# The later router joined into round 2, and the MLP's sums taken out of PSUM ahead of two convolution tiles

## The reference

```python
x = _layernorm(x + _L0_attn_ref(x, ...))   # Mamba-2 mixer, then a gated MLP
x = _layernorm(x + _L0_ffn_ref(x, ...))    # top-2 of 8 experts: softmax router, one matrix and bias each
x = _layernorm(x + _L1_attn_ref(x, ...))   # attention, 16 heads, relative positions
x = _layernorm(x + _L1_ffn_ref(x, ...))    # top-2 of 8 gated experts with a capacity of 512
```

```python
mlp = jax.nn.silu(h @ gate_w.T) * (h @ up_w.T) @ down_w.T
x = x + mlp_scale[None, None, :] * mlp
gate_scores = jax.nn.softmax(jnp.einsum('bsd,ed->bse', x, Wg) + bg, axis=-1)
topk_scores, topk_idx = jax.lax.top_k(gate_scores, 2)
```

## Time and profile before

| | us |
|---|---|
| median of 3 runs | 1363.02 |
| lowest, highest | 1362.93, 1367.55 |
| the profiled execution | 1364.65 |
| its span, first to last instruction | 1362.9 |
| the four slots that the diff touches | about 80 to 500 of the span |
| attention, then second experts | about 500 to 1363 |

### The profile page before, as it was taken

One profiled execution on the slowest core, in us unless ns is written; L12 is line 12 of the kernel. 1 busy time (PEld: TensorE's weight loads), 2 busy tenths in 40 slices (PEclk: granted clock), 3 DMA queues, 4 the chain that ended last, 5 costly groups with the idle time before them and its releaser, 6 DMA issues. The chain is left out here.

```text
span 1362.9 us, 39431 instructions
## 1 busy us (share of the span) xinstructions
PE 1224.1 (90%) x16528; PEld 648.2 (48%) x16528; DVE 1091.9 (80%) x2184; ACT 902.2 (66%) x1739; POOL 295.2 (22%) x417
## 2 busy tenths in 40 slices
PE   4988888889888778999999999999999999994995
PEld 2555445545554423555555444454445544432552
DVE  6777888989785888999999989989899998934123
ACT  5665345537513305999998888888889888891242
POOL 2222131330312015000000200601106011054471
PEclk9999989999898988999999999999999999996998
DMA  5080000200208503102122011302111200011235
GB/s 144 1 234 16 1 2 17 111 2 1 112 1 154 144 1 146 38 21 45 36 56 64 21 37 45 83 27 61 38 44 40 63 13 22 13 43 39 58 101 187
DMA packets 59703, 77.72 MB, mean 57 GB/s; under 512 B 15010, under 2 KB 41189, under 8 KB 57686
## 3 DMA queue, kind: packets, MB, share of 16 engines
q1 hardware_dynamic: 56454, 70.95, 19.4%
q0 software_dynamic: 3072, 4.25, 1.0%
HBM read 37.18 MB, written 40.03 MB: 57 GB/s over the span
## 5 line engine op out<-in xcount | busy, mean ns | idle before, releaser
L1491 ACT ACTIVATE space<-ps 128x512 f32<-128x512 f32 x1024 | 605.4, 598 | 85.9 <-PE ps L671 37.3
L2151 DVE TENSOR_REDUCE smax<-ps 128x1 f32<-128x1024 f32 x512 | 613.6, 1220 | 50.6 <-PE ps L671 26.0
L671 PE MATMUL ps<-space 96*32 96x512 bf16 (+2 forms) x8432 | 614.9, 381 | 23.3 <-DVE smax L2151 12.8
L671 PEld LDWEIGHTS ps<-space 96*32 96x32 bf16 (+2 forms) x8432 | 255.0, 98 | 286.6 <-DVE smax L2151 42.6
L1052 PE MATMUL ps<-space 128*9 128x256 f32 x4096 | 319.6, 379 | 0.0
L1052 PEld LDWEIGHTS ps<-space 128*9 128x9 f32 x4096 | 119.8, 92 | 98.1 <-ACT space L1491 1.0
L1355 ACT ACTIVATE btok<-ps 128x128 f32<-128x128 f32 x32 | 8.9, 278 | 106.1 <-issue 89.6
L2096 DVE SCALAR_TENSOR_TENSOR x<-ps,gsel,x 128x128 f32<-128x128 f32 x256 | 69.0, 342 | 8.0 <-PE ps L671 7.6
L671 PE MATMUL ps<-w_exp,xnT 128*128 128x512 f32 x128 | 63.5, 620 | 13.3 <-DVE x L2096 13.3
L1596 POOL TENSOR_SCALAR eps_sum<-mv 128x4 f32<-128x4 f32 x32 | 7.4, 233 | 314.0 <-DVEq L1867 313.3
L671 PE MATMUL ps<-ones,ident 128*128 128x512 bf16 x228 | 59.0, 419 | 17.4 <-POOLq L1707 12.3
(11 more groups left out here) (250 smaller groups left out, 1416.5 us busy)
## 6 DMA issues: line engine op xcount, KB each, us to landing
head_sums<-space SPq DMA_DIRECT2D x31, 256.0 KB
q_rows<-space SPq DMA_DIRECT2D x24, 256.0 KB, 2.5
k_rows<-space SPq DMA_DIRECT2D x24, 256.0 KB, 2.8
space<-k_rows SPq DMA_DIRECT2D x16, 384.0 KB, 5.4
space<-q_rows SPq DMA_DIRECT2D x16, 384.0 KB, 7.1
expert_out<-x_all SPq DMA_DIRECT2D x2, 2048.0 KB, 18.3
space<-expert_out SPq DMA_DIRECT2D x4, 1024.0 KB, 9.5
v_rows<-space SPq DMA_DIRECT2D x4, 576.0 KB, 3.4
```

Source lines behind the costliest of these rows:

```text
L671: return nc.tensor.matmul(out, lhsT, rhs, start=first, stop=last)
L1491: nc.scalar.activation(prob[:, QUAD * (step % PROB_SETS) + unit % QUAD, :], bank(STB + unit % 2), ACT.Exp)\
L2151: v.tensor_reduce(smax[:, N % 2, i:i + 1], ps[:, b0:b0 + 2, :].rearrange("p k n -> p (k n)"), AX.X, ALU.max).then_inc(S.s_max, 1)
```

## The change

TensorE's `route0` goes from the end of round 1 into round 2, between `chunk_state` and the next chunk's front. ScalarE's `evac_T` for the router goes ahead of `decays_so_far` in round 1. VectorE's `route_logits` and `route_shift` go from round 1 into round 2, ahead of `chunk_weights`; `route_which`, `route_picks` and `gate_parts` go ahead of `chunk_weights` in round 3, and in round 5 (`BIAS_AT`) the first `experts_scaled` does. At the MLP's end VectorE's `skip_rows` goes into the loop at n = 6, both `skip_sum` go ahead of the last two of the left convolution tiles, and the statistics go behind `chunk_inputs` of chunk 0. ScalarE's list behind the loop stays as it was.

```diff
--- before.py
+++ after.py
@@ -963,6 +963,10 @@
                         chunk_carried(m, c)
                         if c < NT - 1:
                             chunk_state(m, c)
+                    if p is not None and c == 2:
+                        route0(p)
+                    if m is not None:
+                        if c < NT - 1:
                             chunk_front(m, c + 1)
                             chunk_after(m, c + 1)
                     if p is not None and c == 1:
@@ -980,8 +984,6 @@
                         if c == NT - 1:
                             mix_out(m, 0)
                     if p is not None:
-                        if c == 1:
-                            route0(p)
                         if c == 2 and m is None:
                             keep_clock(YB, 10)
                             score_pair(0)
@@ -1432,14 +1434,14 @@
                     if m is not None and c < NT - 1:
                         chunk_copy(m, c + 1)
                         chunk_exp(m, c + 1)
+                    if p is not None and c == 1:
+                        evac_T("moe", p, (7, 5))
                     if m is not None and c + 2 < NT:
                         decays_so_far(m, c + 2)
                     if p is not None and c == BIAS_AT:
                         evac_gates(p)
                     if m is not None and c in (2, 4, 6):
                         gated_squares(m, c // 2 - 1)
-                    if p is not None and c == 1:
-                        evac_T("moe", p, (7, 5))
                     if p is not None and c == 2:
                         route_exp(p)
                     if q is not None and c < 3:
@@ -2061,7 +2063,6 @@
                 dve.wait_ge(S.down_psum, 2 * b + H + 1)
                 v.tensor_tensor(xa[:, own(H), :], xa[:, own(H), :], tiles4(5 + H), ALU.add).then_inc(S.skip_sum, 1)
                 dve.wait_ge(S.skip_sum, 2 * b + H + 1)
-                statistics(xa, H, 0)
 
             def gate_parts(b):
                 for k in range(TOPK):
@@ -2169,6 +2170,8 @@
                 for n in range(2 * HID_TILES):
                     if p is not None:
                         hidden(p, n)
+                    if p is not None and n == 2 * HID_TILES - 2:
+                        skip_rows(p)
                     if q is not None and p is not None and n == 0:
                         expert_norm(q, 1)
                     if m is not None and 2 <= n + 1 < conv_in_mlp(q):
@@ -2178,18 +2181,21 @@
                         if p is None and n == 5:
                             for pair in range(EARLY_PAIRS - 3, EARLY_PAIRS):
                                 pair_max(pair)
-                if m is not None:
-                    for j in range(conv_in_mlp(q), N_CONV):
-                        convolve(m, j)
+                late = list(range(conv_in_mlp(q), N_CONV)) if m is not None else []
+                for j in late[:1]:
+                    convolve(m, j)
                 if m == 0:
                     position_parts(1)
                 if p is not None:
-                    skip_rows(p)
+                    for H in range(2):
+                        skip_sum(p, H)
+                for j in late[1:]:
+                    convolve(m, j)
+                if m is not None:
+                    chunk_inputs(m, 0)
                 if p is not None:
                     for H in range(2):
-                        skip_sum(p, H)
-                if m is not None:
-                    chunk_inputs(m, 0)
+                        statistics(xa, H, 0)
                 if q is not None:
                     for H in range(2):
                         evac_keys(q, H)
@@ -2210,13 +2216,19 @@
                             normalise(xa, x2, H, 0, 6 * p + H)
                     if q is not None and p is not None and c in (1, 2):
                         cut_rest(q, c - 1)
+                    if p is not None and c == 2:
+                        route_logits(p, 6, b_route0)
+                        route_shift(p)
+                    if p is not None and c == HT - 1:
+                        route_which(range(NT))
+                        route_picks()
+                        gate_parts(p)
                     if m is not None and p is not None and HT <= c < NT - 1:
                         ahead = SCALED_AT[c][:1]
                     else:
                         ahead = ()
                     for k in ahead:
-                        if c != BIAS_AT:
-                            experts_scaled(p, k)
+                        experts_scaled(p, k)
                     if m is not None and c < NT - 1:
                         chunk_weights(m, c + 1)
                     if m is not None and c == NT - 1:
@@ -2228,19 +2240,12 @@
                         if m + 1 < B:
                             input_norm(m + 1)
                     if p is not None:
-                        if c == 1:
-                            route_logits(p, 6, b_route0)
-                            route_shift(p)
                         if c == 2:
                             route_shares(p)
                             route_best(range(NT))
-                        if c == HT - 1:
-                            route_which(range(NT))
-                            route_picks()
-                            gate_parts(p)
                     if p is not None:
                         for k in SCALED_AT.get(c, ()):
-                            if k not in ahead or c == BIAS_AT:
+                            if k not in ahead:
                                 experts_scaled(p, k)
                             if c == BIAS_AT:
                                 bias_added(p)
```

## The result

The changed kernel takes **1369.06 us** (median of 16 runs, 1366.04 to 1372.47), the kernel before 1364.66 us over 16 runs (1360.1 to 1369.62): a ratio of **1.0032 [1.0021, 1.0044]**. The first three runs of the kernel before had a median of 1363.02; with more runs that moved up by 1.6 us. So the difference was forecast at +1.7 us and measured at +4.4 us. The profiled execution took 1369.76 us (span 1368.0).

A forecast was written before the change was run, and what follows sets the result against it. VectorE was taken to set the pace, its waits being what could be won. A -2.2, B +2.55, C +0.75 and D +0.6 gave +1.7 us on the median of 1363.02: 1364.7 us, range 1359.5 to 1369.5.

The forecast's parts named there:

- same: Whole kernel: a time between 1356.2 and 1369.8 us, not told from no change; chance 0.84.
- the low clock lasts: Rival, B and C: TensorE slow over 7 us after work returns, 2.5 us more each; +6.7, 1369.7 us; chance 0.10.
- The sums wait for the products: MLP's end, B and C: VectorE's two sums wait about 1 and 3 us for the down products.
- ScalarE's kept order holds the queries: B and C: last SiLU waits for the last tile, queries' input behind it; keys +1.7 us in B, -0.1 in C.
- bank 6 is what holds the queries: Rival, B and C: keys come when VectorE's work is done, no slow clock; -6.9 in sum, 1356.1 us; chance 0.05.
- The clock behind the gap: B and C: TensorE idle 5.8 us ahead of the queries, then 1.2 GHz; +2.1 us each.
- the clock stays up: Rival, B and C: no slow clock after the gap, both 2.1 us drop out; 1360.5 us; chance 0.22.
- A's statistics: Slot A: statistics end 1.9 us later, delaying GpSimd's root and decays; VectorE's first hst +1.5 us.
- The router in A: Slot A's rounds: logits' wait of 2.14 us goes, weights' waits are filled by 0.7 and 0.88; -3.7 us.
- the router's joining moves its wait only: Rival, A to C: route0 delays VectorE's inputs, weights' waits reappear, router's gains go; +7.9, 1370.9 us; chance 0.08.
- The router in B and C: Rounds of B and C: 0.4 us of the logits' wait and 0.88 of round 3 go; -1.25 us each.
- The router in D: Slot D: logits now stand behind the second cut_rest, out of the shadow of ScalarE's copies; +0.6 us (0 to 0.8).

The follow-up runs named there:

- the gap filled: Changed kernel plus TensorE products without a reader in its gap ahead of the queries: 1365.14 us (0.9993) in slots B and C, 1362.90 us (0.9975) with A too.
- ScalarE's order changed: Changed kernel with ScalarE's two halves of the queries' input ahead of the last two tiles' SiLU, queries ahead of the very last: 1362.88 us, 0.9980.
- the router alone: Kernel before with only the router's moves, the MLP's end as it was: 1357.91 us, 0.9942.
- the MLP's half: Kernel before with only the MLP's end changed (skip_rows, both sums, statistics), the router as it was: 1374.30 us, 1.0065.
- the whole kernel: Changed kernel with another tile and A's statistics ahead of sums, ScalarE's query work earlier, D's logits at their old place: 1350.56 us, 0.9883.

## Why the prediction was right or wrong

The time fell inside the range and the forecast "same" held, but with +4.4 us where the sum had +1.7. There is luck in it: 1369.06 is 0.44 us below the upper end, the second timing of the same kernel, 1371.72, lies above it, and by the time alone the rival "the low clock lasts" (+6.7) is as near as the forecast. It is the traces that decide for the forecast's mechanism. Step by step:

- **The sums wait for the products**: right. Foreseen about 1 and 3 us; 1.02 and 2.91.
- **ScalarE's kept order holds the queries**: right, to 0.2 us. Foreseen +1.7 us in B, -0.1 in C; with the gap filled they are +1.88 and +0.09. The rival "bank 6 is what holds the queries" is out: with ScalarE's order changed the keys need no wait at all.
- **The clock behind the gap**: right in kind, 1.5 to 2.7 us a slot for 2.1. The row of a 5 us gap was the right neighbour, not B's shorter gaps, so the rival "the clock stays up" falls. The Trainium skill, "TensorE: Matmul & The Clock Gate" (HAM oscillation — how this bites in real kernels), has each burst behind such a wait start at half the clock; the 0.69 of the windows agrees for part of the burst. "The low clock lasts" is out too: the 16 value products right behind the projections took 1.95 us in both slots and both traces, about a quarter of the 7.31 us that 64 of their form take in the earlier trace rows.
- **A's statistics**: a step that failed, by size: +2.82 us for +1.5. It followed GpSimd only to `hdec`, the second of the two decay instructions, which got 0.45 us shorter, and so came to +1.5. But `chunk_state` waits for the first, `xw`, which has no such relief: 2.48 us later, then 0.52 us more of TensorE, less about 0.26 us by which it was ahead of `hdec` before; 2.74 of the 2.82 us measured.
- **The router in A**: -3.7 foreseen, -3.1 to -4.1 in the changed kernel, -3.05 alone. With the router alone faster by 7.9 us, the rival "the router's joining moves its wait only" is out. `experts_scaled(3)` won nothing, as foreseen: a wait of 0.96 us for TensorE stands ahead of the products of round 5 where the weights waited before.
- **The router in B and C**: -1.25 foreseen, -0.45 to -1.53.
- **The router in D**: +0.55 for +0.6 as far as the shares go. But **the step ended there**, and this is the larger failure. D's expert sums were put at nothing, and no reason is given for it; they cost +1.54 and +2.45 us. The sum took each piece that isn't edited at its old duration, and these traces show such pieces at two clocks.

With the last and A's statistics at their measured size (+2.0 on average, +1.3) the sum is 1.7 + 3.3 = +5.0, against +4.4 and +6.4 in the two medians and +5.1 and +5.9 in the two traces.

## What to carry to other kernels

A read of PSUM that an engine's list reaches before the products are done cost the whole remainder here (1.02 and 2.91 us); so count the work that stands ahead of it in each list, and when a read is moved forward move the work that its result lets another engine do, too. Here the MLP's half lost 8.5 us without ScalarE's list and without cover; with both the whole kernel won 14.7 us, of which the router's half alone gives 7.9. A longer wait ahead of TensorE was paid once as a wait and once more in the speed of what follows, and the clock moved stretches that nobody edited as well.

## What the runs showed of the hardware that was not expected

GpSimd's small TENSOR_SCALAR (128x4) took 0.77 us instead of 0.23, and the next one started 0.86 us behind it instead of 0.31, where VectorE started a product of two SBUF tiles in the same moment (121.62, 0.69 us); the second trace and the MLP's end alone show the same 0.77. The Trainium skill, "SBUF — State Buffer" (SBUF: two separate sides), says that such a VectorE instruction and a GpSimd one that reads SBUF shut each other out for a whole instruction; the rows agree: VectorE's ended at 122.31, GpSimd's at 122.39.

The clock of D's expert products changed by an order that is set a few microseconds ahead of them, and not in the same way in each execution: two traces of one kernel had three and two groups at 1.2 GHz, 34.68 and 33.77 us. So one trace of such a stretch is uncertain by about 1 us, an estimate from these two.
